# A two-layer image network on one core: input tiles of their own, a third of a depthwise chunk moved to TensorE, and a new order of all engines

## The chip, the cores and the metric

The kernel runs on one core of one Trainium2 chip. The metric is the device time of one execution in microseconds. Before the change three executions took 6348.39, 6352.19 and 6352.39 us (median 6352.19 us).

## What is computed

32 images of 96 channels and 56 x 56 positions, float32, pass two layers. Each layer is a convolution block and then a feed-forward block, both added to their input:

```python
# layer 0
x = x + L0_conv(ln_c(x))      # 96 -> 576 channels, silu, depthwise 3x3, silu,
                              # squeeze-excite gate, 576 -> 96, and + its own input
t = t + L0_ffn(ln_t(t))       # 96 -> 384 -> 96, fp8 products, relu
# layer 1
x = x + L1_conv(ln_c(x))      # 96 -> 96, group norm over the image, gelu,
                              # 4 shifted copies, each 96 -> 96 and gelu, summed,
                              # group norm over the image, 96 -> 96
t = t + L1_ffn(ln_t(t))       # as L0_ffn
```

`ln_c` and `ln_t` normalise over the 96 channels at each position, a group norm over a whole image. So a convolution block has points at which all of an image must be done: the gate needs the mean of all 576 channels, and each group norm needs its sums.

## The kernel before

Channels lie on partitions, positions along the free dimension. An image is cut into 8 tiles of 392 columns (7 rows). TensorE does every product, in matmuls of 32 output columns: the helper `columns` (L525) issues one for each 32 columns of the weights, so an output of 128 partitions is 4 matmuls that go to 4 column groups of the array, and one of 96 partitions is 3. A float32 matmul stands as two records in the trace.

The 576 channels of layer 0 are four chunks of 128 and one of 64. The depthwise convolution of chunks 0, 1 and 2 is on VectorE: each half image (1568 columns) is 9 steps, one `tensor_scalar` (L875) and eight `scalar_tensor_tensor` (L878), in `dw k h j` (chunk, half, tap). Chunks 3 and 4 are on TensorE, in three units of 4 x 32 channels of a half: `texp u p` expands them into a layout by row phases (L565), a DMA copies a part (`phases_on`), and `tconv u r` (L578, 12 matmuls each) convolves. ScalarE applies silu between (`expand`, `texp`) and after (`silu2`, L760, a half of a chunk at once; `tconv`, L751).

The normalisations go through `center` (TensorE subtracts the mean), squares on ScalarE (L710, L785), `var` (L532, a matmul of 98 columns for each quarter of a tile, that sums the squares of a position into one partition of a PSUM bank), `rstd` (VectorE, an integer seed and two Newton steps, L387 to L412, then 4 DMAs to memory) and `fetch` (a DMA of each tile back, broadcast over partitions). Then `norm` multiplies. Suffix `_a` is the norm ahead of layer 0, 0 and 2 the norms ahead of the feed-forwards, 1 the norm ahead of layer 1. In `var_rows` the four quarters of a tile go to the four partition quadrants:

```python
row = ROW[:, NT - 1 - t:NT - 1 - t + QUAD]
for j in range(VT):
    last = mm(VPS[th][QUAD * j:QUAD * j + QUAD, :], row, sq[:, j * VW:(j + 1) * VW],
              start=(t == 0), stop=(t == NT - 1))
```

A feed-forward tile is `up` (TensorE 12 matmuls; ScalarE copies to float16, L794), `quant` (VectorE bias and relu, 3 instructions, L934; ScalarE rounds to fp8, L801), `down` (TensorE 9 matmuls; ScalarE copies, L808) and `add` (VectorE, L941 and L944). Layer 1 has `conv1`, `stats` and `gn 0`, `gelu1`, `shift` (5 DMAs a tile), `combo` (24 records a tile, gelu L829), `fold`, `sum`, `gn 1`, `conv3` and `x2`. The gate is `se1`, `se2`, `se3`; then `proj` (15 matmuls a tile) and `x1` (VectorE, L905).

Each of the five engines runs its own list in order; semaphores alone tie them. The list is made by `timetable()` out of the table `TIMES`, which gives each step of each engine a number in a frame of 10000; step s of image i stands at frame i + lead(s), so parts of up to four images are under way in one frame. The numbers set the order only. The whole input image is loaded in one DMA (`load_x`) into X, the buffer in which x + norm, the result of layer 0 and the output are made later; `norm_a` on GpSimd (L1021) adds the norm to it and `save_s` stores that sum to memory, from where `fetch_s` brings it for `x1`.

## Time and profile before

| | before |
|---|---|
| median of 3 runs | 6352.19 us |
| profiled execution, its own time | 6357.4 us |
| its span | 6355.6 us |
| VectorE busy | 5427.7 us (85%) |
| TensorE busy (ends modelled) | 5322.0 us (84%) |
| ScalarE busy | 4235.9 us (67%) |
| GpSimd busy | 387.8 us (6%) |
| mean granted TensorE clock | 0.951 |
| DMA, mean | 88 GB/s, 35% of 16 engines |

The span is one execution from the first to the last instruction; the other 1.8 us of the execution's time lie around it. One image follows another every 191.2 us, so the views are best read over one such period; the one used here goes from 2004.9 to 2196.1 us.

### The profile page before, as it was taken

What the parts mean: (1) busy time and instruction counts of PE and PEld (TensorE: products, weight loads), DVE (VectorE), ACT (ScalarE), POOL (GpSimd) and SP (SyncE); (2) the same over time, 40 slices, a digit from 0 to 9 for tenths busy, and PEclk for the clock granted to TensorE, in tenths of its full rate; (3) what the DMA queues carried; (4) which work ended last, traced back from release to release, by engine and by line L of the source; (5) the groups of instructions that cost most, each with busy time, mean ns of one, the idle gap of its engine ahead of it and who ended that gap; (6) DMA issues with size and microseconds to landing.
All of it is one profiled execution on the core that took longest, in us unless ns stands there. A gap on an engine that the chain in (4) does not pass through costs nothing.

```text
span 6355.6 us, 157935 instructions
## 1 busy us (share of the span) xinstructions
PE 5322.0 (84%) x63746; PEld 2302.9 (36%) x63746; DVE 5427.7 (85%) x8977; ACT 4235.9 (67%) x7415; POOL 387.8 (6%) x366
## 2 busy tenths in 40 slices
...
GB/s 44 59 90 96 98 80 93 93 88 93 95 78 94 94 93 94 94 77 93 100 91 93 96 80 93 94 91 93 95 79 93 95 91 96 94 81 92 97 64 69
...
## 3 DMA queue, kind: packets, MB, share of 16 engines
...
## 4 chain that ended last, share of the span: by engine, by line
PE 37%; DVE 33%; ACT 10%; DMA 8%; issue 6%; SPq 5%; POOL 0%; DVEq 0%; ACTq 0%
PE bank L525 19%; DVE conv L878 12%; PE b_banks L681 6%; PE b_banks L525 5%; DMA shifted<-g 4%; DVE hidden L934 4%; DMA r_b<-rstd_row_b 3%; DVE x L944 2%; DVE xn L926 2%; SPq L490 2%; ACT conv L760 2%; PE bank L565 2%; ACT hidden L794 2%; DVE ffn_out L941 2%; DVE bn_stats L949 1%
## 5 line engine op out<-in xcount | busy, mean ns | idle before, releaser
L878 DVE SCALAR_TENSOR_TENSOR conv<-mid,w_dw,conv 128x1568 f32<-128x1568 f32 x1536 | 2877.1, 1873 | 23.8
L525 PE MATMUL bank<-conv,w_proj_gated 128*32 128x392 f32 x7680 | 918.4, 507 | 0.0
L525 PE MATMUL bank<-x,centering 128*32 128x392 f32 x6144 | 847.1, 500 | 20.9 <-ACT mid L733 11.7
L681 PE MATMUL b_banks<-shifted,w_combo 128*32 128x392 f32 x6144 | 653.2, 545 | 234.0 <-DMA shifted<-g 199.4
L525 PE MATMUL bank<-xc_a,w_exp 128*32 128x392 f32 x6144 | 705.2, 501 | 67.2 <-DVE xc_a L861 38.9
L794 ACT ACTIVATE hidden<-b_banks 128x1176 f16<-128x1176 f32 x512 | 594.4, 1161 | 159.5 <-PE b_banks L525 152.3
L733 ACT ACTIVATE mid<-bank 128x392 f32<-128x392 f32 x768 | 388.6, 506 | 387.7 <-PE bank L525 377.2
L801 ACT ACTIVATE hidden<-hidden 128x1176 fp8e5<-128x1176 f16 x512 | 616.3, 1204 | 1.5 <-DVE hidden L934 0.3
L525 PE MATMUL b_banks<-xn,w_q 128*32 128x392 fp8e5 x6144 | 519.9, 335 | 73.6 <-DVE xn L926 54.1
L525 PEld LDWEIGHTS bank<-conv,w_proj_gated 128*32 128x32 f32 x7680 | 357.4, 113 | 457.8 <-issue 448.7
L1021 POOL TENSOR_TENSOR x<-x,xc_a 96x392 f32<-96x392 f32 x256 | 368.2, 1443 | 1863.6 <-DVE xc_a L861 1863.6
L565 PE MATMUL bank<-xc_a,w_exp 128*32 128x448 f32 x3072 | 465.0, 599 | 3.0 <-DVE xc_a L861 1.1
L934 DVE TENSOR_SCALAR hidden<-hidden,b_q 128x392 f16<-128x392 f16 x1536 | 397.6, 313 | 76.6 <-ACT hidden L794 76.6
L578 PE MATMUL bank<-phases_on,w_toeplitz 128*32 128x392 f32 x4608 | 437.1, 493 | 7.9 <-ACT mid L733 7.8
L681 PEld LDWEIGHTS b_banks<-shifted,w_combo 128*32 128x32 f32 x6144 | 211.2, 117 | 604.8 <-DMA shifted<-g 340.3
L525 PE MATMUL bank<-hidden,w_q 128*32 128x392 fp8e5 x4608 | 352.7, 334 | 81.3 <-ACT sq_b L785 46.6
L578 PE MATMUL bank<-phases,w_toeplitz 128*32 128x392 f32 x4608 | 419.6, 494 | 0.1
L525 PE MATMUL b_banks<-g,w_l 128*32 128x392 f32 x1536 | 238.4, 544 | 193.7 <-DVE g L921 193.6
L740 ACT ACTIVATE phases<-bank 128x448 f32<-128x448 f32 x384 | 217.5, 567 | 259.1 <-PE bank L565 259.0
L532 PE MATMUL sums_a<-sq_a,row_select 128*32 128x98 f32 x4096 | 275.0, 253 | 96.5 <-ACT sq_a L710 96.5
L525 PEld LDWEIGHTS bank<-x,centering 128*32 128x32 f32 x6144 | 240.7, 111 | 311.7 <-issue 233.2
L709 ACT ACTIVATE xc<-bank 96x392 f32<-96x392 f32 x256 | 132.3, 517 | 325.1 <-PE bank L525 325.1
...
## 6 DMA issues: line engine op xcount, KB each, us to landing
...
r_b<-rstd_row_b SPq DMA_DIRECT2D x512, 147.0 KB, 2.9
shifted<-g SPq DMA_DIRECT2D x256, 199.5 KB, 2.9
...
r_a<-rstd_row_a SPq DMA_DIRECT2D x256, 147.0 KB, 3.0
x_plus_norm<-x SPq DMA_DIRECT2D x256, 147.0 KB, 2.6
r_a<-x_plus_norm SPq DMA_DIRECT2D x256, 147.0 KB, 2.4
```

Source lines behind the costliest of these rows:

```text
L525: last = mm(o[j:j + QUAD, :], weights[:, j:j + QUAD], x, start=start, stop=stop)
L532: last = mm(VPS[th][QUAD * j:QUAD * j + QUAD, :], row, sq[:, j * VW:(j + 1) * VW], start=(t == 0), stop=(t == NT - 1))
L565: last = mm(ring[bank][32 * q:32 * q + 32, 0:EROWS * WW], WEXP[:, m0:m0 + 32], xc_phase(q, h), start=True, stop=True)
L578: last = mm(ring[bank][32 * p:32 * p + 32, 0:TW], TWZ[:, (3 * g + dx) * 2 + r % 2, :], phase_rows(EB if r < 2 else FB, p, QH, dx), start=( ...
L681: last = mm(rows(PB[32 * u:32 * u + 32, m, 0:TW]), WC[:, u // 2, 32 * m:32 * m + 32], SH[t % 2][:, u, :].rearrange("p (h w) -> p h w", w=G ...
L733: f(mid_rows((k + (k < AHEAD) + parity) % 2, 1 + ROWS * t, ROWS), rows(ring[bank][:, 0:TW]), ACT.Silu)\
L740: f(phase_rows(EB, p, EROWS, 1), rows(ring[bank][:, 0:EROWS * WW]), ACT.Silu)\
L794: f(Y16[t % 2][:, :, :], PB[:, 0:NHC, 0:TW], ACT.Copy).then_inc(sem["up_evacuated"], 1)
L801: f(Q8[t % 2][:, :, :], Y16[t % 2][:, :, :], ACT.Copy, saturate=False)\
L878: v.scalar_tensor_tensor(out=acc, in0=src, scalar=WDW[:, k, j:j + 1], in1=acc, op0=ALU.mult, op1=ALU.add).then_inc(sem["convolved"], 1)
L934: last = v.tensor_scalar(Y16[t % 2][:, c, :], Y16[t % 2][:, c, :], B1Q[:, g, c:c + 1], 0.0, ALU.add, ALU.max)
L1021: g.tensor_tensor(tile(XA, t), tile(XA, t), xc_tile(t), ALU.add).then_inc(sem["xplus_a"], 1)
```

## The change

1. Input tiles. Four buffers `x_in` of one tile each take the input. `load_x` becomes 8 DMAs an image; since a tile is given up once it is centred, each is loaded a second time (`reload_x`, 8 more DMAs) for the sum x + norm, which GpSimd makes in the tile's buffer. X is no longer held by the input.
2. Depthwise. Half 0 of chunk 0 leaves VectorE: `dw 0 0` (9 steps), `silu2 0 0` and three tiles of `expand 0` go, and a fourth unit of `texp` and `tconv` comes, first in the order.
3. The rstd rows. The 32 rows of sums of squares now stand on 32 partitions (96 to 127): all `var` matmuls write that one quadrant, one DMA stores the row in place of 4, and the integer seed is one instruction in place of two.
4. Group norm. The inverse root is one `pow` on GpSimd in place of the seed and Newton steps on VectorE (9 instructions), and the steps (`gn`, `gn_spread`, `gn_var`, `gn_affine`) stand apart in the order so that others come between.
5. Second feed-forward. Its centred input has a buffer of its own (in `shifted`), so tiles 0 to 3 of `up 1`, `quant 1`, `down 1`, `add 1` come before conv1 of the next image and tiles 4 to 7 after it, up to the combos and past them.
6. `TIMES` is new for every step of every engine.

```diff
@@ program, the change cut to its core
-UNITS, SLOTS = 3, 4
-NGR = (MID - NDV * 128) // 32
+UNITS, SLOTS = 4, 4
+NGL = (MID - NDV * 128) // 32
+NGR = NGL + SLOTS
+XSLOTS = 4
+SPLIT = 4
...
-        "dw 0 0": (7259, 7577, 7649, 7764, 8111, 8146, 8285, 8502, 8773),
-        "dw 0 1": (9657, 9826, 9988, 10426, 10577, 10708, 11003, 11031, 11129),
+        "dw 0 1": (8931, 9250, 9378, 9380, 9911, 10004, 10285, 10345, 10570),
...
+    XL = [sb(f"x_in{n}", [128, TW], fp32) for n in range(XSLOTS)]
+    RAFULL = [sb(f"r_a{n}", [128, TW], fp32) for n in range(2)]
+    XC2 = SHFULL[0:C, 0:NPOS]
-    V = {th: sb(f"var_{th}", [VT * QUAD, VW], fp32) for th in "ab"}
+    V, Y, TMP = ({th: RAFULL[n][C:C + VR, j * VW:(j + 1) * VW] for n, th in enumerate("ab")} for j in range(3))
-    VPS = {"a": small_a[:, 0:VW], "c": small_a[:, 128:128 + VW], "b": small_b[:, 0:VW]}
+    VPS = {"a": small_a[C:C + VR, 0:VW], "c": small_a[C:C + VR, 128:128 + VW], "b": small_b[C:C + VR, 0:VW]}
...
+    def ffn(f, image):
+        return NT * (min(2 * image + 2, 2 * NIMG - 1) if f else max(2 * image - 1, 0))
+    fetches = [(frame - (L == 2), L, t) for frame in range(NIMG + 1)
+               for L, tiles in ((0, range(NT)), (2, range(SPLIT)), (1, range(NT)), (2, range(SPLIT, NT)))
+               for t in tiles if 0 <= frame - (L == 2) < NIMG]
...
             if name == "load_x":
-                for t in range(NT):
-                    sp.wait_ge(stored[t], at(16 * b))
-                sp.dma_start(XA[:, :], x[n, :, :]).then_inc(sem["x_loaded"], 16)
+                t = arg[0]
+                if t < XSLOTS:
+                    sp.wait_ge(s_stored[t], at(16 * (NT // XSLOTS * n)))
+                else:
+                    sp.wait_ge(sem["centered_a"], at(NT * n + t - XSLOTS + 1))
+                load_x(sp, n, t)
+            elif name == "reload_x":
+                t = arg[0]
+                if t < XSLOTS:
+                    sp.wait_ge(sem["centered_a"], at(NT * n + XSLOTS + t + 1))
+                else:
+                    sp.wait_ge(s_stored[t % XSLOTS], at(16 * (NT // XSLOTS * n + t // XSLOTS)))
+                load_x(sp, n, t)
...
-            row = ROW[:, NT - 1 - t:NT - 1 - t + QUAD]
             for j in range(VT):
-                last = mm(VPS[th][QUAD * j:QUAD * j + QUAD, :], row, sq[:, j * VW:(j + 1) * VW],
-                          start=(t == 0), stop=(t == NT - 1))
+                r = VT * t + j
+                last = mm(VPS[th], ROW[:, VR - 1 - r:VR - 1 - r + QUAD], sq[:, j * VW:(j + 1) * VW],
+                          start=(r == 0), stop=(r == VR - 1))
...
+            elif name == "root":
+                pool.wait_ge(sem["gn_vector"], at(GN_V * (2 * b + arg[0] + 1)))
+                g.tensor_tensor(col(GY), col(GV), HALVED[:, :], ALU.pow).then_inc(sem["gn_rstd"], 1)
```

What stands now where is seen at three places. First VectorE from the gate on, through the projection. Before (L999 are the `sum` steps, L890 and L892 the gated weights, L1003 `x2`, L905 `x1`, `conv_0` is half 0 of chunk 0):

```order
L890 TENSOR_TENSOR w_proj_gated<-w_proj,gate 128x480
L892 TENSOR_SCALAR w_proj_gated<-w_proj,gate 64x96
L999 BN_STATS bn_stats<-g 96x6 x2
L966 BN_AGGR gn_small<-bn_stats 96x2
...
L875 TENSOR_SCALAR conv_0<-mid,w_dw 128x1568
L1003 SCALAR_TENSOR_TENSOR x<-b_banks,gn_small,x 96x392
L861 TENSOR_TENSOR xc_a<-xc_a,r_a 96x392
L1003 SCALAR_TENSOR_TENSOR x<-b_banks,gn_small,x 96x392 x3
L861 TENSOR_TENSOR xc_a<-xc_a,r_a 96x392
L1003 SCALAR_TENSOR_TENSOR x<-b_banks,gn_small,x 96x392
L878 SCALAR_TENSOR_TENSOR conv_0<-mid,w_dw,conv_0 128x1568 x3
L1003 SCALAR_TENSOR_TENSOR x<-b_banks,gn_small,x 96x392
```

Of the change (L955 and L957 the gated weights, L1059 `x2`, L965 `x1`, L940 and L943 depthwise steps):

```order
L955 TENSOR_TENSOR w_proj_gated<-w_proj,gate 128x480
L957 TENSOR_SCALAR w_proj_gated<-w_proj,gate 64x96
L1059 SCALAR_TENSOR_TENSOR x<-b_banks,gn_small,x 96x392
L965 SCALAR_TENSOR_TENSOR x<-bank,bn_bias,r_a 96x392 x2
L1059 SCALAR_TENSOR_TENSOR x<-b_banks,gn_small,x 96x392
L965 SCALAR_TENSOR_TENSOR x<-bank,bn_bias,r_a 96x392 x5
L940 TENSOR_SCALAR conv_1<-mid,w_dw 128x1568
L965 SCALAR_TENSOR_TENSOR x<-bank,bn_bias,r_a 96x392
L943 SCALAR_TENSOR_TENSOR conv_1<-mid,w_dw,conv_1 128x1568
L1059 SCALAR_TENSOR_TENSOR x<-b_banks,gn_small,x 96x392
```

The depthwise steps that stood among `x2` and `x1` are gone; the gate now comes after gn 1, and the first depthwise step after seven of the eight `x1`.

Second, TensorE at the same place. Of the change (L577 is `columns`, L631 `tconv`, L584 `var`):

```order
L577 MATMUL bank<-conv,w_proj_gated 32x392 x12
L577 MATMUL bank<-x,centering 32x392 x3
L631 MATMUL bank<-phases,w_toeplitz 32x392 x12
L584 MATMUL sums_a<-sq_a,row_select 32x98 x4
L577 MATMUL bank<-conv_1,w_proj_gated 32x392 x3
L577 MATMUL bank<-conv,w_proj_gated 32x392 x12
L584 MATMUL sums_a<-sq_a,row_select 32x98 x4
L577 MATMUL bank<-x,centering 32x392 x6
L584 MATMUL sums_b<-sq_b,row_select 32x98 x4
```

The first `tconv` of the new unit stands inside the projection, and each `var` stands between matmuls of 96 output partitions.

Third, ScalarE in the combos. Before (L829 and its table loads, L733 `expand`, L751 and L760 the second silu, L833 `fold`):

```order
L829 ACTIVATE gelus<-b_banks 128x392 x3
L751 ACT_TABLE_LOAD
L751 ACTIVATE conv,pool_sums<-bank,bn_affine 128x7x56
L833 ACTIVATE g<-bank 96x392 x2
L829 ACT_TABLE_LOAD
L829 ACTIVATE hidden<-b_banks 128x392 x3
L829 ACTIVATE gelus<-b_banks 128x392 x3
L733 ACT_TABLE_LOAD
L733 ACTIVATE mid<-bank 128x7x56
L760 ACTIVATE conv,pool_sums<-conv,bn_affine 128x1568
L829 ACT_TABLE_LOAD
```

Of the change (L894 the gelus, L864 and L871 the second feed-forward, L898 `fold`, L812 and L823 the second silu):

```order
L894 ACTIVATE gelus<-b_banks 128x392 x3
L864 ACTIVATE hidden<-hidden 128x1176
L871 ACTIVATE ffn_out<-bank 96x392 x2
L898 ACTIVATE g<-bank 96x392
L864 ACTIVATE hidden<-hidden 128x1176
L894 ACTIVATE hidden<-b_banks 128x392 x3
L886 ACTIVATE g<-g,gn_small 96x14x56
L894 ACTIVATE gelus<-b_banks 128x392 x3
L812 ACT_TABLE_LOAD
L812 ACTIVATE conv,pool_sums<-bank,bn_affine 128x7x56
```

The second feed-forward's steps, which need no table of their own, now lie among the gelus; the program has 220 table loads, it had 311.

## Rows read from the trace of the kernel before

**Rows 1.** The page, part 1: busy time, share of the span, instructions.

```profile
PE 5322.0 (84%) x63746; PEld 2302.9 (36%) x63746; DVE 5427.7 (85%) x8977; ACT 4235.9 (67%) x7415; POOL 387.8 (6%) x366
```

**Rows 2.** Busy time by stage: stretch, its length, then busy and instructions, PEclk, DMA, GB/s.

```profile
2004.90:2015.90 11.00, 10.67 (x156) 5.42 (x147) 10.62 (x24) 10.22 (x18) 0.00 (x0) 1.00 0.26 76
2015.90:2052.90 37.00, 32.40 (x465) 14.04 (x462) 36.55 (x70) 34.06 (x56) 0.00 (x0) 1.00 0.27 69
2052.90:2062.10 9.20, 7.59 (x92) 2.71 (x84) 8.82 (x15) 4.49 (x9) 0.00 (x0) 1.00 0.29 73
2062.10:2086.50 24.40, 19.50 (x208) 8.35 (x208) 20.35 (x25) 14.78 (x31) 0.31 (x3) 0.86 0.47 108
2086.50:2138.30 51.80, 38.83 (x425) 14.41 (x418) 46.66 (x64) 40.62 (x69) 9.43 (x6) 0.93 0.56 128
2138.30:2142.80 4.50, 3.36 (x17) 1.41 (x20) 2.92 (x18) 0.72 (x2) 0.00 (x0) 0.66 0.43 117
2142.80:2196.10 53.30, 52.95 (x648) 24.79 (x646) 41.59 (x68) 27.00 (x51) 2.04 (x2) 1.00 0.26 66
sum 191.20, PE 165.30 PEld 71.12 DVE 167.51 ACT 131.89 POOL 11.78; mean PE 23.61 PEld 10.16 DVE 23.93 ACT 18.84 POOL 1.68
```

**Rows 3.** Groups by line and shape: count, busy us and mean ns, idle before.

```profile
L878 DVE SCALAR_TENSOR_TENSOR conv<-mid,w_dw,conv 128x1568 f32<-128x1568 f32 x1536 | 2877.1, 1873 | 23.8
L875 DVE TENSOR_SCALAR conv<-mid,w_dw 128x1568 f32<-128x1568 f32 x192 | 197.7, 1030 | 1.7 <-ACT mid L733 1.7
L401 DVE TENSOR_TENSOR gn_small<-gn_small 96x1 f32<-96x1 f32 x64 | 10.0, 156 | 2.2
```

**Rows 4.** Timeline of VectorE in the first feed-forward: start, us, instruction.

```profile
2020.18 0.78 DVE L934 TENSOR_SCALAR hidden<-hidden,b_q 128x392 f16<-128x392 f16 x3
2020.87 0.32 DVE L941 TENSOR_SCALAR ffn_out<-ffn_out,b_q 96x392 f16<-96x392 f16 x1
2021.22 0.56 DVE L944 TENSOR_TENSOR x<-x,ffn_out 96x392 f32<-96x392 f32 x1
2021.71 0.56 DVE L926 TENSOR_TENSOR xn<-xc,r_b 96x392 fp8e5<-96x392 f32 x1
2022.18 1.84 DVE L878 SCALAR_TENSOR_TENSOR conv<-mid,w_dw,conv 128x1568 f32<-128x1568 f32 x1
```

**Rows 5.** Timeline of TensorE, at several places: start, us, matmul records.

```profile
2009.56 4.16 PE L578 MATMUL bank<-phases,w_toeplitz 128*32 128x392 f32 x48
...
2154.90 3.49 PE L525 MATMUL bank<-conv,w_proj_gated 128*32 128x392 f32 x30
2158.19 0.53 PE L525 MATMUL bank<-x,centering 128*32 128x392 f32 x3
```

**Rows 6.** Timeline of TensorE, `center` and `var` in turn.

```profile
2151.44 0.53 PE L525 MATMUL bank<-x,centering 128*32 128x392 f32 x3
2151.48 0.36 PE L532 MATMUL sums_b<-sq_b,row_select 128*32 128x98 f32 x2
2151.77 0.53 PE L525 MATMUL bank<-x,centering 128*32 128x392 f32 x3
2152.09 0.37 PE L532 MATMUL sums_b<-sq_b,row_select 128*32 128x98 f32 x6
```

**Rows 7.** SyncE's DMA issues in the combos: first of one tile's five and first of the next tile's.

```profile
2091.89 0.64 SPq L486 DMA_DIRECT2D shifted<-g  x1
...
2095.26 0.60 SPq L486 DMA_DIRECT2D shifted<-g  x1
```

**Rows 8.** The page, part 6: DMA issues, KB each, us to landing.

```profile
x_plus_norm<-x SPq DMA_DIRECT2D x256, 147.0 KB, 2.6
```

**Rows 9.** Timeline of VectorE at the end: last rstd of the last image, then its first norm.

```profile
6321.40 0.26 DVE L403 SCALAR_TENSOR_TENSOR rstd_b<-newton_b,rstd_b 128x98 f32<-128x98 f32 x1
6326.55 0.56 DVE L926 TENSOR_TENSOR xn<-g,r_b 96x392 fp8e5<-96x392 f32 x1 [4.88 <-DMA r_b<-rstd_row_b]
```

**Rows 10.** Groups by line: the largest of the five that load ScalarE's tables.

```profile
L829 ACT ACT_TABLE_LOAD x124 | 159.1, 1283 | 34.2 <-PE b_banks L681 32.5
```

More of the change, by code:

```diff
@@ L49 @@
     "SP": {
-        "load_x": (3080,), "rstd_a": (4972,), "fetch_a": (5306, 5426, 5508, 5710, 5827, 6103, 6321, 6510),
-        "save_s": (6383, 6573, 6610, 6759, 6784, 7012, 7108, 7757), "texp 0": (6651, 9964, 10173, 10430),
-        "texp 1": (11021, 11243, 12055, 12182), "texp 2": (13398, 14087, 14481, 14553),
-        "fetch_s": (16809, 17796, 17831, 18100, 18379, 19362, 19839, 19924), "rstd 0": (20402,),
-        "fetch 0": (20453, 20569, 20851, 20898, 20927, 20986, 21263, 22031), "rstd 1": (22588,),
@@ L55 @@
-        "fetch 1": (22625, 22632, 23484, 23545, 24219, 24310, 24444, 24474),
-        "shift": (24602, 24905, 25247, 25389, 25390, 25433, 25479, 25804), "rstd 2": (28097,),
-        "fetch 2": (28422, 29587, 29616, 29629, 29701, 29923, 29957, 30012),
-        "store": (30127, 30403, 30850, 31022, 31112, 31134, 31518, 31747),
+        "load_x": (-1046, 1593, 1707, 2485, 3098, 3212, 3528, 3832),
+        "reload_x": (4583, 4683, 4860, 6926, 7306, 8157, 8490, 9355), "rstd_a": (5613,),
+        "fetch_a": (5640, 5657, 6154, 6249, 6605, 6927, 7249, 7331),
@@ L127 @@
+        "root 1": (28036,),
     },
```

344 lines of the change are left out of this document (193 added, 151 removed), and 100 rows, old and new, of the table TIMES.

## The prediction

> **What bounds the kernel now.** I read the page first, then the stages of one period, then the timelines in each stage. VectorE is busy 85% of the span and TensorE 84% [rows 1]; neither share says which of them binds, because they bind in turn. The view by stages cuts one period of 191.2 us [rows 2] at points that both programs have: the start of rstd 0, the first norm 0, rstd 1, the first norm 1, gn 0 (its `bn_aggr`), gn 1, the scaling of the conv3 weights, and rstd 0 again. In the seven stages VectorE is busy 10.6 of 11.0, 36.6 of 37.0, 8.8 of 9.2, 20.4 of 24.4, 46.7 of 51.8, 2.9 of 4.5 and 41.6 of 53.3 us; TensorE is busy 53.0 of 53.3 in the last [rows 2]. So for 134 us of the period VectorE binds (with 8 us of waits), and for 53 us TensorE does, while it works off proj, conv3 and the centrings; there VectorE's depthwise steps fill its gaps. Work taken off VectorE pays only in the first six stages, work put on TensorE costs at once in the seventh.
>
> **Unit times.** By start to start in a timeline [rows 4], a `quant` takes 0.70 us on VectorE, an `add` 0.83 (0.35 + 0.49), a `norm` 0.48; a depthwise step is 1.87 us busy, 1.77 start to start where GpSimd is idle, and 0.96 for the first of nine [rows 3, 4]; the next instruction starts some 0.08 before a record ends. I take 0.54 for `x1` and `x2` and 0.48 for `stats` and `sum`, an estimate from the 0.48 of `norm`, with the same tile, and one PSUM operand more. On TensorE 48 records of `tconv` take 3.95 us (the record's 4.16 less the drain), so a `tconv` r of 24 is 1.97, or 0.33 us for each 392-column record of a column group, and an `expand` tile of 8 is 0.66; a `proj` tile is 3.29 (2154.90 to 2158.19), 10 passes of 0.33, and a 96-wide tile of 6 records 0.66 too [rows 5].
>
> **What the change removes, adds and moves, an image.**
> - VectorE loses `dw 0 0`: 8 x 1.873 + 1.030 = 16.0 us busy [rows 3]. The root of the group norm takes 9 instructions of 0.156 twice, 2.8 us [rows 3]; one seed instruction of about 0.25 goes four times, 1.0 us. Together 19.8 of 167.5: 148 remain.
> - TensorE loses three `expand` tiles (2.0) and gains 4 `texp` of 448 columns (0.66 x 448 / 392 = 0.75 each, 3.0) and 4 `tconv` (7.9): +8.9 us.
> - `var`: 32 tiles of 8 records of 98 columns, a quarter of 392, so 0.082 each. Four groups side by side they take 2 x 0.082 = 0.16 us a tile; in one group 8 x 0.082 = 0.65. Whether the other 0.49 is lost depends on TensorE's order between groups. The trace shows it: the program has all 6 centring records ahead of the `var`, yet two `var` records start at 2151.48, before the last three centring records at 2151.77 [rows 6]. These two are of the group that centring does not use, and that is the group in which all of `var` now stands. So I take `var` as hidden beside the 96-wide tiles around it, which saves 0.16 x 32 = 5 us for groups 0 to 2; bounds are that gain and 0.49 us a tile. The Trainium skill (page "TensorE: Matmul & The Clock Gate", section "The mechanism") says the contrary, that matmuls start and end in strict program order. By it each `var` would block what follows. The trace disagrees [rows 6], but not for 8 records in one group, so it is a rival below.
> - ScalarE: minus 3 `expand` and a `silu2`, plus 4 `texp` and 4 `tconv`, +2.4 us; 91 fewer table loads of 1.283 [rows 10], -3.6. It is busy 132 of 191 [rows 2]: no term, beyond the combos.
> - GpSimd: two `pow` on 96 x 1. Nothing in the trace has it; the nearest are L401's 0.16 and the whole chain it replaces (1.4), so 0.2 to 2 us. VectorE has an `add` or a `norm_a` to do meanwhile: 0 taken.
> - SyncE: 15 more input DMAs, 12 fewer of rstd rows, 8 more of the new unit. An issue takes 0.65 us (the five of a shift tile, 3.37 us from one first to the next [rows 7]), so it has some 95 of 183 us to issue. What counts is what it waits for, below.
>
> **Stage by stage.** The method, tried on before: the second stage holds 8 norm, 8 quant, 8 add of the first feed-forward, 1 quant and 4 add of the second, and 10 depthwise steps of which one is a first: 3.8 + 6.3 + 10.0 + 0.96 + 9 x 1.77 = 37.0, and 37.0 were measured [rows 2]. The new lists give:
> 1. rstd 0 to norm 0: rstd 2.5, 2 taps, a first tap, 2 `x2` = 8.1 (11.0 before). The transfer hides under it: from the last rstd to the first norm 5.2 us pass with nothing else to do [rows 9], and now three issues fewer.
> 2. to rstd 1: 8 norm 0, 3 norm 2, 9 quant, 8 add, rstd 2, 12 taps and a first: 3.8 + 1.4 + 6.3 + 6.6 + 2.5 + 21.2 + 1.0 = 42.9 (37.0). More depthwise stands here than before.
> 3. to norm 1: 2.5 + 3 taps 5.3 + 0.7 + 0.5 = 9.0 (9.2).
> 4. to gn 0: 8 norm, 8 stats, 4 taps, a first, 2 quant, 2 add, 2 norm 2 = 19.7, and half of the 4.0 of waits that stand there now [rows 2], since there is more to do between: 21.7 (24.4).
> 5. to gn 1: 16 taps at 1.85 (the slower mean of this stage), a first, 4 quant, 4 add, 2 norm, rstd_a, 5 norm_a, 8 sums and 1.9 of group norm = 48.2, with 1 of waits 49.2 (51.8). Beside it SyncE's 8 shift tiles take 8 x 3.4 = 27 us, and the combos with their chain some 45; ScalarE has the second feed-forward among the gelus (10 us) but 4 to 5 table loads less.
> 6. to gn_weights: 3.3 (4.5).
> 7. to rstd 0: now a chain. The gate stands after the sums: two `silu2` halves of 1.8, se1 to se3 and the gated weights put proj 0 about 8 us behind gn_weights (conv3 and center 2 run meanwhile). Then TensorE: 8 proj 26.4, 8 center 0 5.3, 3 center 2 and 2 conv3 3.3, 3 expand 2.0, the new `tconv 0 0` 2.0 = 39.0, and 1.5 to the sums: 48.8 (53.3). VectorE has only some 25 us of work here and idles.
>
> The sum is 183.0, that is 8.2 us less an image. Half of the 16 us taken from VectorE pays, the other half becomes idle time in stage 7. 32 x 8.2 = 262 us; start and end (237 us beyond 32 periods) I leave as they are. Against the profiled execution, 6357.4 - 262 = 6095; the median of before lies 5 under it: **6090 us**.
>
> **The rivals.**
> - **No waits.** Stage 4 without 2, stage 5 with taps at 1.77 and no wait (-2.3), stages 6 and 7 with 4 less, since TensorE's clock no longer falls to 0.93 and 0.66 before the projection [rows 2] with the second feed-forward in those gaps: 174.7, 16.5 less, 5830. For it speaks that the work is there; against it, that waits stand in each of these stages today.
> - **`var` blocks.** By strict order 0.49 us for each of 11 `var` tiles in stage 7, 5.4 us, the other 21 in stages where TensorE has slack of 2 to 13 us: 188.4, 6263. This is the skill page's rule as a time.
> - **SyncE's line, slower than before.** Each store of x + norm must land (2.6 us [rows 8]) before `reload_x` 5 and 6 and the next `load_x` 0 go, and they stand between `fetch_s` 5 and 6, behind which x1 6, center 0 and rstd 0 wait: 3 x 2.6 and 10 issues of 0.65 are 14.3 us, and 2.6 for `fetch_s` 6 to land, against 11 us of projection between x1 3 and x1 6 (3 proj and 2 center): 5.9 us. If the same happens at the `load_x` 4 to 7 ahead of `fetch 1` and `fetch 2` (each waits for a centring, an estimate of 4 x 1.5, a `norm` and a `conv1` tile each), the sum is 11.9: 194.9, 6470. It decides from 8.2 us of such waits an image. Against it: the first two stores can land while texp copies are issued, and x1 lags no bank until both of its buffers are used.
> - **The change does not do what it says:** VectorE's idle time just moves, the same period, 6352. It would need another stage to grow by 8 us with its units unchanged.
>
> **How the numbers follow.** Forecast 0.45, no waits 0.25, `var` blocks 0.15, SyncE 0.10, nothing 0.05. A measurement of this kernel tells 0.2% (13 us) from no change. Faster is the first three and some of the last, 0.87; same 0.03; slower 0.10. The range takes in the no-waits case but for its best end and the `var` case: 5860 to 6280; it leaves out the SyncE case and the lower edge.
>
> **What would show it.** Right: a period of 183 us; VectorE's busy time near 4800 us (148 x 32 and some 60), and in stage 7 about 25 of 49 us; TensorE full there; depthwise steps x1280; stage 2 near 43 us; two or more `var` records among each centring. Wrong: `var` records 0.08 apart with no centring record between, so that stage 7 is 54; VectorE waiting for `r_a<-x_plus_norm` in `x1` by more than 1 us an image; a wait of VectorE for GpSimd's `pow`; ScalarE over 90% busy in the combos. A period over 191 would make the stages wrong altogether.

## The result, and the profile after

The changed kernel takes 6085.89 us (median of 4 runs, 6082.74 to 6089.76), the kernel before 6350.29 us beside it (4 runs): ratio 0.959, 95% interval 0.9571 to 0.9608. The forecast was 6090. The profiled execution has a span of 6080.9 us and a mean granted clock of 0.97.

The page of the changed kernel, part 1 (busy time, share, instructions), as in [rows 1]:

```profile
PE 5405.2 (89%) x67266; PEld 2754.9 (45%) x67266; DVE 4828.3 (79%) x7988; ACT 4189.5 (69%) x7517; POOL 505.0 (8%) x431
```

Busy time by stage for one period of 182.9 us, the seven stages of [rows 2] in the same order (the columns are PE, PEld, DVE, ACT, POOL, PEclk, DMA, GB/s):

```profile
2087.70:2096.00 8.30, 8.30 (x118) 4.48 (x113) 7.93 (x15) 3.54 (x10) 0.00 (x0) 1.00 0.19 59
2096.00:2139.00 43.00, 42.40 (x613) 25.18 (x608) 42.38 (x77) 39.41 (x68) 0.00 (x0) 1.00 0.34 90
2139.00:2148.10 9.10, 9.10 (x127) 4.70 (x122) 8.76 (x18) 8.44 (x15) 0.00 (x0) 1.00 0.16 37
2148.10:2167.60 19.50, 18.84 (x245) 9.57 (x238) 19.43 (x34) 17.31 (x36) 0.31 (x3) 1.00 0.56 145
2167.60:2216.10 48.50, 38.34 (x438) 17.66 (x432) 47.50 (x70) 43.91 (x70) 8.12 (x3) 0.93 0.68 165
2216.10:2222.10 6.00, 3.07 (x28) 0.96 (x28) 4.38 (x10) 4.40 (x9) 3.72 (x4) 1.00 0.14 25
2222.10:2270.60 48.50, 48.25 (x564) 24.21 (x568) 18.88 (x30) 13.70 (x34) 3.04 (x3) 0.96 0.28 78
```

TensorE is now full in stages 1, 2, 3 and 7, and in the first three VectorE is nearly full too. VectorE has 30 of its 34 us of idle time in stage 7, where it waits for projections; the group has both this and the wait for a transfer that one rival was about:

```profile
L943 DVE SCALAR_TENSOR_TENSOR conv<-mid,w_dw,conv 128x1568 f32<-128x1568 f32 x1280 | 2337.2, 1844 | 3.9
L965 DVE SCALAR_TENSOR_TENSOR x<-bank,bn_bias,r_a 96x392 f32<-96x392 f32 x256 | 159.2, 622 | 772.4 <-PE bank L577 757.2 <-DMA r_a<-x_plus_norm 15.2
```

The 256 fewer depthwise steps are 8 an image. The waits for x + norm are 15.2 us in all, 0.5 an image.

Stage 6 is the only one where the forecast was far too short (6.0 us against 3.3); stage 4 was forecast 2.1 us too long. VectorE's timeline in stage 6, then GpSimd's:

```profile
2219.14 0.97 DVE L1038 TENSOR_TENSOR gn_small<-gn_small,v_l 96x1 f32<-96x1 f32 x1 [0.44 <-POOL gn_small L1076]
2220.15 0.94 DVE L1040 TENSOR_TENSOR gn_small<-gn_small 96x1 f32<-96x1 f32 x1
2221.11 0.93 DVE L1042 TENSOR_TENSOR gn_small<-v_l,gn_small 96x1 f32<-96x1 f32 x1
2222.08 0.27 DVE L1046 TENSOR_SCALAR w_scaled<-w_l,gn_small 96x96 f32<-96x96 f32 x1
```

```profile
2218.31 0.80 POOL L1076 TENSOR_TENSOR gn_small<-gn_small,minus_half 96x1 f32<-96x1 f32 x1 [14.93 <-DVE gn_small L1030]
2219.08 2.95 POOL L1082 TENSOR_TENSOR x_in<-x_in,xc_a 96x392 f32<-96x392 f32 x3
```

The `pow` takes 0.80 us and costs VectorE 0.44 us of waiting. But GpSimd's queue has three x + norm adds behind the second root. They start the moment the root is done, 0.98 us each, and each of the three steps on 96 x 1 now takes as long as one of them, where 0.16 is their time [rows 3]. The Trainium skill has a reason (page "SBUF — State Buffer", section "Who interferes with whom"): a VectorE instruction with two SBUF inputs contends with a GpSimd instruction that reads SBUF, for a shared read interface, and the page calls the shared ports an exclusive lock. These rows agree: each step lasts about as long as one add.

To see every image, not one, I took the starts of `rstd 0`, the first `norm 0`, `rstd 1`, the first `norm 1`, the two `bn_aggr` and the scaling of the conv3 weights from VectorE's timelines of each profiled execution, and averaged the stages over 26 to 28 images in the middle of the run (us):

| kernel | 1 | 2 | 3 | 4 | 5 | 6 | 7 | period |
|---|---|---|---|---|---|---|---|---|
| before | 11.1 | 37.0 | 9.3 | 23.6 | 52.3 | 4.4 | 53.4 | 191.0 |
| forecast | 8.1 | 42.9 | 9.0 | 21.7 | 49.2 | 3.3 | 48.8 | 183.0 |
| changed | 8.3 | 43.1 | 9.1 | 19.6 | 48.7 | 6.0 | 47.7 | 182.4 |

Stage 7 of the changed kernel has two lengths, 47.0 us in 15 of 27 images and 48.6 in 12. The first 6 us of that stage in two neighbouring images, each with the 6 us ahead of it:

```profile
2034.70:2040.70 6.00, 3.06 (x28) 0.96 (x28) 4.38 (x10) 4.42 (x9) 3.73 (x4) 1.00 0.15 28
2040.70:2046.70 6.00, 5.74 (x89) 3.67 (x92) 4.64 (x13) 1.34 (x4) 0.00 (x0) 1.00 0.12 35
2216.10:2222.10 6.00, 3.07 (x28) 0.96 (x28) 4.38 (x10) 4.40 (x9) 3.72 (x4) 1.00 0.14 25
2222.10:2228.10 6.00, 5.75 (x74) 3.04 (x75) 4.10 (x10) 0.74 (x3) 0.00 (x0) 0.72 0.13 41
```

In the long images the mean granted clock is 0.72 there, that is 1.2 GHz for part of the stretch and 2.4 GHz for the rest, after 6 us in which TensorE was busy half of the time; in the short ones it is 1.00 after the same 6 us. This is so in all 27: 0.72 in the 12 long ones, 1.00 in the others. It costs 1.5 us.

### The profile page after: what moved, and what is told of

It reads as the page before. It is cut to its first block, busy times and chain, and to the rows that moved or that the text cites. A ratio compares the mean times of both kernels' runs of the same rounds, so it can differ in the third digit from the quotient of the medians.

```text
span 6080.9 us, 165237 instructions
## 1 busy us (share of the span) xinstructions
PE 5405.2 (89%) x67266; PEld 2754.9 (45%) x67266; DVE 4828.3 (79%) x7988; ACT 4189.5 (69%) x7517; POOL 505.0 (8%) x431
## 4 chain that ended last, share of the span: by engine, by line
DVE 38%; PE 27%; issue 25%; POOL 4%; DMA 3%; ACT 1%; SPq 1%; DVEq 0%; POOLq 0%; ACTq 0%
PE bank L577 18%; DVE conv L943 16%; DVE hidden L994 4%; POOL x_in L1082 4%; DVE xn L986 3%; PE sums_a L584 2%; PE b_banks L577 2%; DVE g L981 2%; DMA x_in<-in_x 2%; DVE bn_stats L1009 2%; DVE x L1004 2%; PE bank L631 1%; DVE conv L940 1%; DVE ffn_out L1001 1%; PE sums_b L584 1%
## 5 line engine op out<-in xcount | busy, mean ns | idle before, releaser
L943 DVE SCALAR_TENSOR_TENSOR conv<-mid,w_dw,conv 128x1568 f32<-128x1568 f32 x1280 | 2337.2, 1844 | 3.9
L577 PE MATMUL bank<-conv,w_proj_gated 128*32 128x392 f32 x7680 | 872.0, 493 | 0.5 <-DVE w_proj_gated L957 0.5
L965 DVE SCALAR_TENSOR_TENSOR x<-bank,bn_bias,r_a 96x392 f32<-96x392 f32 x256 | 159.2, 622 | 772.4 <-PE bank L577 757.2
L577 PE MATMUL bank<-xc_a,w_exp 128*32 128x392 f32 x5376 | 690.5, 498 | 69.4 <-ACT mid L794 34.9
L577 PE MATMUL bank<-x,centering 128*32 128x392 f32 x4608 | 637.1, 500 | 11.0 <-DVE x L1004 9.1
L631 PE MATMUL bank<-phases,w_toeplitz 128*32 128x392 f32 x6144 | 634.0, 492 | 0.0
L864 ACT ACTIVATE hidden<-hidden 128x1176 fp8e5<-128x1176 f16 x512 | 604.5, 1181 | 38.5 <-DVE hidden L994 38.5
L631 PE MATMUL bank<-phases_on,w_toeplitz 128*32 128x392 f32 x6144 | 629.5, 492 | 0.4 <-DMA phases_on<-phases 0.4
L577 PE MATMUL b_banks<-xn,w_q 128*32 128x392 fp8e5 x6144 | 463.8, 348 | 177.0 <-ACT hidden L857 104.1
L1082 POOL TENSOR_TENSOR x_in<-x_in,xc_a 96x392 f32<-96x392 f32 x256 | 443.1, 1744 | 2025.0 <-DMA x_in<-in_x 1098.8
L577 PEld LDWEIGHTS bank<-conv,w_proj_gated 128*32 128x32 f32 x7680 | 314.9, 110 | 503.6 <-issue 481.7
L584 PE MATMUL sums_a<-sq_a,row_select 128*32 128x98 f32 x4096 | 453.6, 256 | 2.0 <-ACT sq_a L768 1.9
L812 ACT ACTIVATE conv<-bank,bn_affine 128x392 f32<-128x392 f32 x512 | 344.6, 674 | 156.9 <-PE bank L631 156.0
L767 ACT ACTIVATE shifted<-bank 96x392 f32<-96x392 f32 x256 | 125.7, 491 | 460.3 <-PE sums_b L584 299.2
L584 PE MATMUL sums_b<-sq_b,row_select 128*32 128x98 f32 x4096 | 431.8, 249 | 3.6 <-ACT sq_b L768 1.9
```

The source lines that it names most:

```text
L577: last = mm(o[j:j + QUAD, :], weights[:, j:j + QUAD], x, start=start, stop=stop)
L584: last = mm(VPS[th], ROW[:, VR - 1 - r:VR - 1 - r + QUAD], sq[:, j * VW:(j + 1) * VW], start=(r == 0), stop=(r == VR - 1))
L631: last = mm(ring[bank][32 * p:32 * p + 32, 0:TW], TWZ[:, (3 * g + dx) * 2 + r % 2, :], phase_rows(EB if r < 2 else FB, p, QH, dx), start=( ...
L812: f(conv_rows(u, r), rows(ring[bank][:, 0:TW]), ACT.Silu, scale=SCB[:, 0, k:k + 1], bias=SCB[:, 1, k:k + 1], accum_out=SUMS[:, j:j + 1]).t ...
L864: f(Q8[t % 2][:, :, :], Y16[t % 2][:, :, :], ACT.Copy, saturate=False)\
L943: v.scalar_tensor_tensor(out=acc, in0=src, scalar=WDW[:, k, j:j + 1], in1=acc, op0=ALU.mult, op1=ALU.add).then_inc(convolved, 1)
```

## The experiments

The stages of the runs made from the changed kernel, by the same method. The runs were taken in several sets, each with the kernel before beside it, whose median lay between 6345.7 and 6359.1 us; so times of different sets are compared to some 10 us, and ratios or stages tell more. All of these kernels but e_pool, e_rootv, e_pool2, e_pool3 and e_pool4 leave out a part of the result.

| kernel | 1 | 2 | 3 | 4 | 5 | 6 | 7 | period | median, us |
|---|---|---|---|---|---|---|---|---|---|
| changed | 8.26 | 43.06 | 9.05 | 19.60 | 48.73 | 5.98 | 47.72 | 182.41 | 6085.9 |
| e_var4 | 8.25 | 43.74 | 9.05 | 19.67 | 48.84 | 5.99 | 49.64 | 185.19 | 6163.3 |
| e_pool | 8.25 | 43.07 | 9.05 | 19.61 | 49.30 | 3.61 | 48.03 | 180.92 | 6040.3 |
| e_rootv | 8.28 | 43.06 | 9.06 | 19.59 | 50.44 | 4.58 | 47.06 | 182.06 | 6083.8 |
| e_proj | 8.25 | 43.06 | 9.05 | 19.57 | 49.04 | 5.98 | 42.91 | 177.87 | 5939.8 |
| e_pool2 | 8.27 | 43.06 | 9.06 | 19.66 | 49.04 | 3.63 | 47.06 | 179.78 | 6002.2 |
| e_pool3 | 8.25 | 43.06 | 9.05 | 19.64 | 48.56 | 3.77 | 47.04 | 179.39 | 5991.1 |
| e_tap4 | 8.26 | 42.87 | 9.05 | 19.58 | 48.34 | 6.14 | 47.68 | 181.93 | 6068.7 |
| e_pe | 8.28 | 43.06 | 9.05 | 19.64 | 52.45 | 6.14 | 48.12 | 186.76 | 6220.3 |
| e_both | 8.27 | 42.36 | 9.05 | 19.71 | 52.51 | 6.14 | 48.00 | 186.05 | 6199.2 |
| e_pool4 | 8.27 | 43.07 | 9.05 | 19.58 | 52.71 | 3.78 | 47.05 | 183.51 | 6121.6 |
| e_gelu | 8.27 | 42.85 | 9.05 | 19.61 | 47.50 | 6.14 | 48.76 | 182.18 | 6072.4 |

**The variance sums back in four column groups (e_var4).**

```diff
-                last = mm(VPS[th], ROW[:, VR - 1 - r:VR - 1 - r + QUAD], ...
-                          start=(r == 0), stop=(r == VR - 1))
+                last = mm(SUMS4[th][QUAD * j:QUAD * j + QUAD, :], ROW[:, VR - 1 - r:VR - 1 - r + QUAD], ...
+                          start=(t == 0), stop=(t == NT - 1))
```

> The changed kernel with one part undone: the 8 records of each variance sum go to four column groups again (two each), as before the change, and no longer all into the fourth. VectorE's root chain still reads only the fourth group's 32 rows, so three quarters of each sum are left out (and the constant under the root is 1.0, so that the values stay finite). TensorE issues the same records. Theory (records of the fourth group run beside centring, projection and feed-forward records of groups 0 to 2, so in one group they cost nothing, and spread over four they take 2 x 0.082 = 0.16 us of groups 0 to 2): up to 32 tiles x 0.16 = 5 us an image if all were on the path, but only the 11 tiles of stage 7 are, 1.8 us, so +0 to +58 us against the changed kernel (6086 to 6144). Rival (matmuls start and end in strict program order, so a tile in one group blocks the rest for 0.65 us, in four for 0.16): 0.49 x 11 = 5.4 us less an image, -173 us (5913).

It took 6163.3 us, ratio to before 0.9694 (0.968 to 0.9709) against 0.959: slower by 77 us (66 by the ratios), where strict order asked for 173 us less. TensorE's timeline of the changed kernel shows the same thing: eight `var` records run in two fours within 0.9 us, each four beside centring records.

```profile
2251.03 0.51 PE L577 MATMUL bank<-x,centering 128*32 128x392 f32 x3
2251.05 0.53 PE L584 MATMUL sums_b<-sq_b,row_select 128*32 128x98 f32 x4
2251.36 0.51 PE L577 MATMUL bank<-x,centering 128*32 128x392 f32 x3
2251.42 0.50 PE L584 MATMUL sums_b<-sq_b,row_select 128*32 128x98 f32 x4
2251.69 0.84 PE L577 MATMUL bank<-x,centering 128*32 128x392 f32 x6
```

The size was more than expected: 1.9 us more in stage 7 and 0.7 in stage 2. In the images of this run where stage 7 begins at a clock of 1.00 it takes 48.1 us, 1.1 more than 47.0; the rest is that 22 of 27 images begin it at 0.72 (49.6 us) or 0.50 (50.9), against 12.

**The x + norm adds behind the second group norm (e_pool).** One wait on GpSimd ahead of the third add:

```diff
                 t = arg[0]
+                if t == 2:
+                    pool.wait_ge(sem["gn_affine"], at(GN_P * (2 * b + 2)))
                 pool.wait_ge(sem["normed_a"], at(NT * n + t + 1))
```

> The changed kernel with one wait more: GpSimd's third x + norm add of an image stands behind the second group norm's last affine step, so the three adds that now run right behind the second root no longer run beside VectorE's three steps on 96 x 1. Theory (these steps took 0.97, 0.94 and 0.93 us in the profile where they take 0.16 without GpSimd beside them, and conv3 and x2 hang on them): 2.4 us less an image in the stage from gn 1 to gn_weights, -75 us (6010), that stage 3.6 us long. Rival (something else would hold the weights or the stage behind gives it back, or the later x + norm stores delay the reloads of x + norm that x1 waits for): 0 or some us more. If the adds then slow the gate's weights or x2 instead, part of it: -30.

6040.3 us, 0.9502 (0.9488 to 0.9516). Stage 6 lost 2.4 us, to the decimal what the three steps lost; the adds now start right behind them, beside what comes next:

```profile
2209.01 0.16 DVE L1038 TENSOR_TENSOR gn_small<-gn_small,v_l 96x1 f32<-96x1 f32 x1 [0.44 <-POOL gn_small L1076]
2209.20 0.15 DVE L1040 TENSOR_TENSOR gn_small<-gn_small 96x1 f32<-96x1 f32 x1
2209.39 0.16 DVE L1042 TENSOR_TENSOR gn_small<-v_l,gn_small 96x1 f32<-96x1 f32 x1
2209.58 1.12 DVE L1046 TENSOR_SCALAR w_scaled<-w_l,gn_small 96x96 f32<-96x96 f32 x1
```

So the contention moved by one instruction (1.12 us instead of 0.27) and stage 7 takes 48.0 us (48.4 in one image). The clock is 1.00 at its beginning in all 27, so of the two lengths only the shorter is left, plus 1.0. Stage 5 grew by 0.6 us, and no run shows why; a period is 1.5 us shorter, not 2.4.

**The roots on VectorE again (e_rootv).**

```diff
-                dve.wait_ge(sem["gn_rstd"], at(q + 1))
+                vector_seed(col(GY), col(GV), "gn_vector", GN_V * q + 4)
+                dve.wait_ge(sem["gn_vector"], at(GN_V * q + 6))
+                vector_newton(col(GY), col(GV), col(GT), "gn_rstd", NEWT * q)
```

> The changed kernel with one part undone: the roots of both group norms are taken by VectorE again, with the seed and the seven Newton steps, and GpSimd has no pow. Counting VectorE's instructions alone: 8 x 0.156 = 1.25 us more twice an image, against 0.44 to 0.8 us of waiting for the pow: +0.5 to +0.8 us each, +30 to +50 us (6116 to 6136). Rival (the cost of the pow is what it does to GpSimd's order: the three x + norm adds stand behind the second root and run beside VectorE's small steps; without the pow they run earlier, beside depthwise steps): the stage from gn 1 to gn_weights loses 2.4 and gains 0.8 us, -50 us (6036), with some of it given back by slower depthwise steps in the stage before.

6083.8 us, 0.9568 (0.9554 to 0.9583): no difference from the changed kernel that these intervals show. Both theories had a part: stage 6 lost 1.4 us and stage 7 0.66 (its clock is 1.00 in all images), but stage 5 took 1.7 more, where the Newton steps of the first root and the freed adds now stand beside depthwise steps. Moving the roots to GpSimd, as it was made, gained nothing net.

**One projection pass left out (e_proj).**

```diff
-                for k in range(NCH):
+                for k in range(NCH - 1):
                     columns(o, WPS[:, k, :], tile(conv(k, t // NTH), ...
```

> The changed kernel with the fourth of the five channel chunks left out of the projection: 8 tiles x 0.66 us = 5.3 us less TensorE work an image, all in stage 7 (gn_weights to rstd 0). Theory (TensorE is what the changed kernel is bound by there, busy 48.25 of 48.5 us): the stage falls to 43.3 us and the time by 32 x 5.3 = 170 us (5916). Rival (the stage hangs on the chain of gate, x1, centring and the loads of x + norm through SyncE's line, with x1 waiting once for a DMA): the stage falls by under 2 us, under -64 us.

5939.8 us, 0.9342 (0.9327 to 0.9358): -146 us. Stage 7 fell by 4.8 of the 5.3 us taken out; the others stayed, but for 0.3 us more in stage 5. TensorE binds stage 7. The next holder shows already. VectorE's waits over the whole run, of the changed kernel, then of e_proj (us in all, times, longest):

```profile
DVE x L965 <- DMA r_a<-x_plus_norm: 15.2, 5, 3.5
```

```profile
DVE x L965 <- DMA r_a<-x_plus_norm: 120.7, 36, 5.7
```

That is the transfer of SyncE's line, in 28 of 30 images.

**VectorE's work taken out of the kernel before, in place (b_nodw).** Eight of nine steps of `dw 0 0` are cut to one column:

```diff
                     dve.wait_ge(sem["convolved"], at(before + j))
+                    if (k, h) == (0, 0):
+                        src, acc = src[:, 0:1, 0:1], acc[:, 0:1, 0:1]
```

> The kernel before, with eight of the nine depthwise steps of chunk 0's first half cut to one column (their products are left out), 8 x 1.77 = 14 us of VectorE's work an image, and nothing put on TensorE for them: the removal on VectorE's side alone. They stand in the stage from gn_weights to rstd 0. Theory (TensorE binds there, busy 53.0 of 53.3 us, so what is taken from VectorE in place is worth nothing; the change gains only since other work fills that stage's room or leaves it): 0 to -1 us an image, 6318 to 6350 us. Rival (VectorE's work is what the whole kernel hangs on, as its 85% say, so it is worth its full time wherever it stands): 14 x 32 = 448 us less, 5902.

6338.4 us, 0.9977 (0.9964 to 0.999), so 14 us (0.2%) for some 390 us of VectorE's time (12.3 an image). Stage 7 of one image, from a profiled execution of 6312.2 us, the shortest of the ten:

```profile
2117.70:2171.60 53.90, 53.55 (x656) 25.01 (x654) 29.33 (x70) 27.51 (x51) 2.04 (x2) 1.00 0.25 66
```

VectorE is busy 29.3 us in it instead of 41.6 [rows 2], and the stage is as long as before. What the change takes off VectorE is worth next to nothing where it stood.

**Adds moved to where VectorE waits (e_pool2, e_pool3).** For e_pool2 the wait is on the first projection tile; for e_pool3 it stands ahead of the first add instead of the third, and the orders of GpSimd and SyncE are moved to match:

```diff
+                if t == 2:            # e_pool3: t == 0
+                    pool.wait_ge(sem["projected"], at(NT * a + 1))
...
-        "norm_a": (7380, 7563, 10331, ...
+        "norm_a": (8040, 8045, 10331, ...
-        "save_s": (6928, ...
+        "save_s": (7690, ...
-        "reload_x": (..., 6926, 7306, 8157, ...
+        "reload_x": (..., 6926, 8082, 8157, ...
```

> The changed kernel; GpSimd's third x + norm add of an image (and so the two behind it) waits until the first projection tile is done, some 9 us into the stage from gn_weights to rstd 0, where VectorE mostly waits. With the wait only behind the group norm (6040 us) the three adds fell into the first 3 us of that stage, where the scaling of the conv3 weights then took 1.12 instead of 0.27 us and an add of the feed-forward 1.08 and 1.26 instead of 0.31 and 0.56; that stage took 48.0 us in every image, 1.0 more than the 47.0 of the changed kernel's shorter images. Theory (that 1.0 is the contention with the adds): the stage takes 47.0, the one before it 3.6, a period of 179.9, 6008 us. Rival (the adds are late now for the stores, so x1 6 waits for its x + norm, or the reloads and the next image's first loads come late): 48 or more, 6040 or slower.

> As the kernel before it in this set, but all x + norm adds of an image wait for the first projection tile, the first two as well; in SyncE's order the first store of x + norm goes from ahead of the loads of x + norm for x1 to behind the fourth of them, and the reload of tile 4 to behind the second store. Theory (the two adds now beside depthwise steps and beside an add of the feed-forward, 1.08 and 1.26 instead of 0.31 and 0.56, cost VectorE 1.0 to 1.5 us in the stage from gn 0 to gn 1, since VectorE binds there): 1.0 to 1.5 us less an image than with three adds moved, -32 to -48 us, 5970 to 5990 if that one is at 6008. Rival (SyncE's line: the first store, its landing of 2.6 us and the reload stand between the loads that x1 waits for; or GpSimd's eight adds end too late): slower than with three adds moved by up to 5 us an image.

e_pool2 took 6002.2 us (0.9453, 0.944 to 0.9466), e_pool3 5991.1 (0.9435, 0.9422 to 0.9449). Stage 7 is 47.0 in both (47.7 in one image of e_pool2), as forecast; moving the first two adds too gave 0.4 us a period rather than 1.0 to 1.5. GpSimd's timeline of e_pool3, the root and then the first four adds, these beside VectorE's waits:

```profile
2368.29 0.81 POOL L1076 TENSOR_TENSOR gn_small<-gn_small,minus_half 96x1 f32<-96x1 f32 x1 [46.74 <-DVE gn_small L1030]
2380.33 3.96 POOL L1084 TENSOR_TENSOR x_in<-x_in,xc_a 96x392 f32<-96x392 f32 x4 [11.23 <-PE bank L577]
```

e_pool3 is the fastest version here that leaves nothing out (e_proj is faster, but lacks a part of the projection), 95 us under the changed kernel: a period 3.0 us shorter, of which 2.2 in stage 6, 0.7 in stage 7 (the clock) and 0.2 in stage 5.

**Four depthwise steps cut (e_tap4).**

```diff
                     dve.wait_ge(convolved, at(taps(m, k, h) + j))
+                    if (k, h) in ((1, 1), (2, 0)) and j in (3, 4):
+                        src, acc = src[:, 0:1, 0:1], acc[:, 0:1, 0:1]
```

> The changed kernel with four of VectorE's 45 depthwise steps cut to one column (their products are left out, about 0.1 us each stays): the fourth and fifth of chunk 1's second half, which stand in the stage from norm 0 to rstd 1, and those of chunk 2's first half, in the stage from gn 0 to gn 1. Theory (VectorE binds in both): 2 x (1.77 - 0.1) = 3.3 us less in the first (43.1 to 39.8) and 2 x (1.85 - 0.1) = 3.5 in the second (48.7 to 45.2), 6.8 x 32 = 218 us, 5868. Rival for the first (TensorE is busy 42.4 of 43.0 us there and binds as well): 0 to 1 us there. Rival for the second (the chain combos, gelus, fold, shift copies, with ScalarE busy 43.9 of 48.5): 0 to 1.5 there, the waits growing by the rest. Nothing in other stages.

6068.7 us, 0.956 (0.9547 to 0.9573). The theory fell: 17 us instead of 218. Stage 2 lost 0.2 us, stage 5 0.4, for 3.1 us of busy time in each (a step on one column still takes 0.21 us). Stages 2 and 5 of one image:

```profile
2266.80:2309.60 42.80, 42.34 (x615) 25.07 (x608) 39.31 (x77) 39.46 (x68) 0.00 (x0) 1.00 0.35 91
...
2338.60:2386.30 47.70, 37.53 (x434) 17.22 (x429) 44.42 (x70) 42.94 (x70) 6.48 (x3) 0.93 0.69 167
```

Most of VectorE's 3.1 us in each stage became waits, for ScalarE's `down` evacuation in stage 2 and, in stage 5, for a row of rstd and for `fold` evacuations:

```profile
2304.36 0.32 DVE L1003 TENSOR_SCALAR ffn_out<-ffn_out,b_q 96x392 f16<-96x392 f16 x1 [2.37 <-ACT ffn_out L871]
...
2380.62 0.56 DVE L926 TENSOR_TENSOR xc_a<-xc_a,r_a 96x392 f32<-96x392 f32 x1 [0.75 <-DMA r_a<-rstd_row_a]
2385.70 0.56 DVE L1057 BATCH_NORM_STATS2 bn_stats<-g 96x6 f32<-96x392 f32 x1 [1.34 <-ACT g L898]
```

**The other side, and both (e_pe, e_both), and fewer table loads (e_pool4).** e_pe and e_both leave out two of three column shifts of `tconv 1`; all three move one Toeplitz output and one half of a silu ahead, and with them two table loads go:

```diff
-                for dx in range(3):
+                shifts = (1,) if u == 1 else (0, 1, 2)
+                for dx in shifts:
...
-        "tconv 3": (13845, 14476, 15566, 16049), "silu2 1": (15581, 16048), ...
+        "tconv 3": (13845, 14476, 15566, 15567), "silu2 1": (15581, 15582), ...
```

> The changed kernel with work taken from the engines beside VectorE, and none from VectorE: in the Toeplitz convolution of unit 1 the products of two of the three column shifts are left out (32 records, 32 / 4 x 0.33 = 2.6 us of TensorE an image, in the stage from norm 0 to rstd 1), and among the combos ScalarE does the last Toeplitz output and the second half of chunk 1's silu right behind the third output and the first half, so two table loads of 1.28 us an image go (2.6 us, in the stage from gn 0 to gn 1). Theory after the run with four depthwise steps cut (3.3 and 3.5 us of VectorE's work were worth 0.2 and 0.4 us in these stages): in both stages VectorE and the others are bound at the same time, so this side alone is worth 0 to 0.5 us in each too, 6055 to 6086. Rival (TensorE alone binds the first, ScalarE's line the second, and VectorE is merely busy): 2.6 us in each, 5920.

> Both at once: the four depthwise steps cut to one column, two of three column shifts of the Toeplitz unit 1 left out, and two table loads fewer among the combos. Theory (both sides bind together): now 2.6 us less in the stage from norm 0 to rstd 1 (43.1 to 40.5) and 2 to 3 in the one from gn 0 to gn 1 (48.7 to 46), where each side alone gave under 0.5: some 5 us an image, 160 us, 5920. Rival (something third holds the stages: a DMA, the gate of buffers, the order of one queue): under 1 us in each, 6050.

> The kernel with all x + norm adds behind the first projection tile (5991 us), and two table loads fewer among the combos. VectorE has 0.5 us of slack more there than in the changed kernel. Theory (both sides bind together there): 0 to 0.7 us less an image, 5970 to 5991. Rival (ScalarE's line alone binds there): 2.6 x 32 = 83 us less, 5908. Against: the two halves and two outputs in one go hold ScalarE for some 7 us, in which no gelu of the combos runs, so up to 1 us an image more is possible, 6023.

6220.3, 6199.2 and 6121.6 us (0.9799, 0.9766, 0.9642; intervals within 0.0014 of each). The expectations count the records left out wrongly: a matmul stands as two records, so 64 go an image and not 32 (the two groups of `tconv` have x5120 records each instead of x6144), by the same 0.33 us 5.3 us and not 2.6. TensorE's busy time in stage 2 fell from 42.4 to 38.2 us. So 4.2 us of TensorE alone are worth 0.00 there, the taps alone 0.19, both 0.70. The stage has a third holder beside these two. In e_both TensorE waits there for ScalarE's `down` and `up` evacuations and centring squares (0.5 to 1.3 us each) and for one `norm` (0.7), ScalarE being busy 39.2 of 42.3: the line of the feed-forward through three engines, in fixed order. I had expected 2.6.

In stage 5 the edit cost 3.7 to 4.2 us where I expected a gain or at most 1 more. Timelines of e_pool4 there, ScalarE, then TensorE:

```profile
2211.21 1.28 ACT L812 ACT_TABLE_LOAD   x1
2212.51 0.68 ACT L812 ACTIVATE conv<-bank,bn_affine 128x392 f32<-128x392 f32 x1
...
2217.69 1.28 ACT L894 ACT_TABLE_LOAD   x1
2218.98 1.28 ACT L894 ACTIVATE hidden<-b_banks 128x392 f32<-128x392 f32 x3
```

```profile
2213.33 0.52 PE L577 MATMUL bank<-hidden,w_q 128*32 128x392 fp8e5 x6 [2.05 <-ACT conv L812]
...
2215.82 0.83 PE L749 MATMUL bank<-gelus,fold 128*32 128x392 f32 x6
2219.62 5.72 PE L739 MATMUL b_banks<-shifted,w_combo 128*32 128x392 f32 x48 [2.97 <-ACT hidden L894]
```

From 2211.2 to 2219.0 no gelu runs. TensorE waits 2.0 us for a bank that the Toeplitz output behind the table load holds, and 3.0 us for the gelus that free the combos' banks. Then 48 combo records take 5.7 us at a granted clock of 0.72, where 24 of them take 2.2 otherwise. The mean granted clock of the stage is 0.90, against 0.93. Busy time fell by 2 us on ScalarE and the stage grew by 4. That these waits and the clock are the whole of it is read from one image's timeline; no run takes them apart.

**Shorter gelus (e_gelu), on top of e_tap4.** The `fold` matmuls behind them work on half of the columns too.

```diff
-                    f(T[t % 2][:, m, :], PB[:, m, 0:TW], ACT.Gelu)
+                    f(T[t % 2][:, m, 0:TW // 2], PB[:, m, 0:TW // 2], ACT.Gelu)
```

> The changed kernel with the four depthwise steps cut to one column as before, and the combos' gelus and folds over half of their columns (196 of 392; the other half of the folded tile is left out): 24 gelus an image of 0.50 us, some 0.38 start to start, become some 0.2 shorter each, 4 to 5 us less on ScalarE in the stage from gn 0 to gn 1; the order of every queue and the table loads stay. With the four steps alone that stage took 48.3 us (48.7 before them), ScalarE busy 42.9, with TensorE's combos waiting for gelus (0.53, 1.33 us) and for the shift copies (0.64, 0.71). Theory (the stage is held by VectorE's work, 44.4 us once two steps are out, and by ScalarE's line of gelus, in which each combo tile waits for the gelus of the tile before it, both at once): 48.3 falls to 45 or 46, -70 to -100 us against the kernel with the steps alone (5970 to 6000). Rival 1 (the shift copies through SyncE and the DMA queues hold the combos): 47.5 or more, under -30 us. Rival 2 (the rest of ScalarE's line, the second feed-forward and the silus, in fixed order): in between, with the waits before gelus gone and others in their place.

6072.4 us, 0.9568 (0.9553 to 0.9584): no faster than e_tap4. The theory fell: ScalarE is busy 3.5 us less in stage 5, and the stage lost 0.8 us, which is rival 1's bound; stage 7 took 1.1 more. TensorE's waits over the whole run, of e_tap4, then of e_gelu (us in all, times, longest):

```profile
PE b_banks L739 <- DMA shifted<-g: 64.0, 73, 7.2
PE b_banks L739 <- ACT hidden L894: 63.5, 67, 2.6
```

```profile
PE b_banks L739 <- DMA shifted<-g: 128.2, 125, 7.2
...
PE b_banks L739 <- ACT hidden L894: 53.5, 48, 1.5
```

The wait for gelus fell by 10 us and the one for the shift copies rose by 64. By these waits the shift copies stand right behind ScalarE. And with less for TensorE to do in stage 5, 23 of 27 images begin stage 7 at a clock of 0.72 or 0.50; in stage 7 those at 0.72 take 48.4 to 48.8 us and those at 0.50 49.8 to 50.0, against 47.0 at 1.00.

## Why the prediction was right, and where it was not

- **The sum.** The period was forecast as 183.0 and is 182.4. From the first scaling of conv3's weights to the last but one, 30 periods, the profiled executions differ by 255 us (5721.9 less 5466.8), 8.5 a period, where the forecast has 8.2. For 32 periods that makes 272 of the 275 us between the spans, so start and end, which I left alone, moved by some 3. That 6090 lies 4 us from the time measured is in part luck: stages 4, 5 and 7 were forecast 3.7 us too long, and stages 1, 2, 3 and 6 3.1 too short.
- **Stage 7, TensorE as its bound.** Right, shown by e_proj (4.8 of 5.3 us) and b_nodw (next to nothing for VectorE's time). VectorE is busy 18.9 us there, where I wrote 25. The 48.8 fits the long images; without the clock's fall it is 47.0. The stretch of 134 us that I gave to VectorE has 10.4 us of its waits in it by [rows 2], not 8; no term of the sum hangs on that.
- **`var` hidden beside centring.** Right: shown by e_var4 and by the records. The Trainium skill's rule that matmuls start and end in strict program order (page "TensorE: Matmul & The Clock Gate", section "The mechanism") doesn't hold here for records in another column group: by it e_var4 would have been faster, and it was 77 us slower.
- **Stages 1 to 3, by VectorE's list.** The numbers hold to 0.2 us (8.1, 42.9, 9.0 for 8.3, 43.1, 9.1), but the reason behind stage 2 is only half true. VectorE is full there, and so are TensorE and the feed-forward's line. The method gives a lower bound; in the kernel before the slack beside it was 4.6 us of TensorE, now it is 0.6. I read "VectorE binds" off a full busy row; e_tap4 shows that its work is worth 0.2 of 3.1 us.
- **Stage 4.** "Half of the waits" was too cautious: 19.6 against 21.7. VectorE is busy 19.4 of 19.5 us, and the granted clock is 1.00 instead of 0.86. That is the part of the no-waits rival that came true; its other parts did not (stage 5 has its 1 us of waits and 0.93).
- **GpSimd, "0 taken".** This is the step that failed. I asked what waits for the `pow` and not what stands behind it in GpSimd's queue. VectorE does wait for the `pow`, 15.2 us in all, which I had named as a sign of being wrong; but that is the small part. The steps after the root took 2.84 us instead of 0.47; with the clock's fall behind them and the two adds in stage 5, that is the 95 us between the changed kernel and e_pool3. It put 2.7 us on stage 6, a third of the gain forecast, and other terms that were too long hid it.
- **ScalarE in the combos.** It is busy 43.9 of 48.5 us, over the 90% that I had called a sign of being wrong. It doesn't hold that stage alone: 3.5 us less of its work gave 0.8 us (e_gelu). The change went further in table loads than I wrote: the trace has 189, not 220, against 311 before.
- **SyncE's line.** It is there as a wait for x + norm in 5 images, 0.5 us an image on average, far from 5.9. But it stands close: with the projection 5.3 us shorter (e_proj) it is 4.0 us an image. In stage 5 the shift copies are the next holder by the waits of e_gelu.
- **Not tried:** the input buffers of their own, the single row of rstd and the spread of the second feed-forward were not undone by themselves, so how much of the 264 us each part of the change gives is not shown. That the spread fills stage 4 and keeps its clock is read from the profile, not shown by a run. Which link of the feed-forward's line holds stage 2 is open too.
